# First stage of an RWKV + MoE kernel: whole projections over four PSUM banks instead of halves over two

## The reference

```python
# attention (RWKV time mix)
prev = xn shifted by one step in time
xk, xv, xr, xg = xn + (prev - xn) * tm_k, tm_v, tm_r, tm_g
r = xr @ Wr.T;  k = xk @ Wk.T;  v = xv @ Wv.T;  g = sigmoid(xg @ Wg.T)
wkv = scan over time of exp(k), exp(k) * v with a decay per channel
o = (sigmoid(r) * wkv * g) @ Wo.T, then a layer norm
# ffn: RMS norm to z, a router (softmax, top 4 of 32 experts, at most 256 tokens each),
# the experts' gated MLPs, and a shared gated MLP of width 1408
```

## Time and profile before

| | |
|---|---|
| median of 3 runs | 1800.13 us (1799.75 to 1804.7) |
| the profiled execution | 1803.59 us, its span 1801.8 us |
| busy over the span | PE 94%, DVE (VectorE) 69%, POOL 49%, ACT 37% |
| mean granted clock of TensorE | 0.979 |
| first stage | 0 to about 484 us |
| second and third stage | to about 949 us, and to the end |

### The profile page before, as it was taken

The page is one execution under the profiler, slowest core; times in us unless marked ns, Lnnn a source line. Parts: engine busy times, 40 slices in busy tenths (PEclk is TensorE's granted clock), DMA queues, the critical chain, the costliest instruction groups (busy, mean ns, idle before and its releaser), DMA issues. The chain is left out here.

```text
span 1801.8 us, 26943 instructions
## 1 busy us (share of the span) xinstructions
PE 1687.4 (94%) x8752; PEld 1445.2 (80%) x8752; DVE 1247.5 (69%) x1798; ACT 661.2 (37%) x1083; POOL 874.2 (49%) x727
## 2 busy tenths in 40 slices
PE   4899999999599999999986889999999999999998
PEld 4687887778489999999974778888788888888887
DVE  4888787888255555555545868778686868777776
ACT  3444445444256656656642322112121211212121
POOL 2678777777634444454423524344252524334251
PEclk9999999999889999999998999999999999999999
DMA  6233334333366676676637655455454443343431
GB/s 222 94 137 129 133 140 160 120 117 117 120 249 217 242 249 221 234 251 228 228 110 263 211 203 170 156 187 172 165 165 140 151 147 106 113 163 117 141 107 51
DMA packets 130475, 299.43 MB, mean 166 GB/s; under 512 B 23692, under 2 KB 35212, under 8 KB 129872
## 3 DMA queue, kind: packets, MB, share of 16 engines
q1 hardware_dynamic: 110928, 264.64, 41.5%
q0 software_dynamic: 19456, 33.67, 6.6%
HBM read 233.64 MB, written 81.36 MB: 175 GB/s over the span
## 5 line engine op out<-in xcount | busy, mean ns | idle before, releaser
L738 PE MATMUL pj<-mix,w 128*128 128x512 f32 x1536 | 368.4, 397 | 18.6 <-POOL mix L311 18.4
L738 PEld LDWEIGHTS pj<-mix,w 128*128 128x128 f32 x1536 | 287.6, 190 | 85.2 <-POOL mix L311 14.6
L1616 PE MATMUL s_gp<-s_zT,s_wg 128*128 128x512 f32 x1056 | 263.7, 400 | 37.6 <-DVE s_wg L1524 21.9
L1616 PEld LDWEIGHTS s_gp<-s_zT,s_wg 128*128 128x128 f32 x1056 | 203.9, 194 | 84.4 <-DVE s_wg L1524 24.8
L1630 PE MATMUL s_yp<-s_wd,s_h 128*128 128x512 f32 x1056 | 255.2, 391 | 2.9 <-DVE s_h L1433 2.9
L1616 PE MATMUL s_up<-s_zT,s_wu 128*128 128x512 f32 x1056 | 253.7, 389 | 0.0
L1630 PEld LDWEIGHTS s_yp<-s_wd,s_h 128*128 128x128 f32 x1056 | 199.2, 189 | 44.7 <-issue 3.3
L1616 PEld LDWEIGHTS s_up<-s_zT,s_wu 128*128 128x128 f32 x1056 | 198.2, 188 | 41.4
L876 POOL TENSOR_TENSOR e_wg<-e_g_in,e_wg 128x1408 fp32r<-128x1408 f32 x32 | 103.4, 3233 | 214.6 <-ACT e_wg L896 214.6
L311 POOL TENSOR_TENSOR mix<-mixf,mix 128x512 fp32r<-128x512 f32 x128 | 175.8, 1403 | 61.1 <-ACT mix L385 60.9
L1275 POOL DMA_INDIRECT s_picked<-y_rows,s_slot x128 | 143.4, 1121 | 85.0 <-DVE s_total L1483 47.4
(11 more groups left out here) (148 smaller groups left out, 2377.5 us busy)
## 6 DMA issues: line engine op xcount, KB each, us to landing
s_wu<-wu_split SPq DMA_DIRECT2D x77, 512.0 KB, 3.5
e_g_in<-in_w_gate SPq DMA_DIRECT2D x32, 704.0 KB, 4.5
e_u_in<-in_w_up SPq DMA_DIRECT2D x32, 704.0 KB, 5.9
zT_tiles<-zT SPq DMA_DIRECT2D x32, 512.0 KB, 2.6
e_d_in<-in_w_down SPq DMA_DIRECT2D x32, 512.0 KB, 6.8
y_rows<-e_y SPq DMA_DIRECT2D x32, 512.0 KB, 2.9
s_zT<-zT_tiles SPq DMA_DIRECT2D x32, 512.0 KB, 5.6
x_in<-in_x SPq DMA_DIRECT2D x32, 256.0 KB, 4.1
```

Source lines behind the costliest of these rows:

```text
L738: last = pe.matmul(pj[m][:], w[i][:, w_part, k, m * P:(m + 1) * P], mix[:, i % 2, k, x_part, :], start=(k == 0 and q == 0), stop=(k == KC ...
L1616: last = pe.matmul(bank[:], parts[w_part][:, k, :], zT[:, :, x_part, k, :], start=(q == 0 and k == 0), stop=(q == 2 and k == KC - 1))
```

## The change

On TensorE `project` no longer takes a half. Chunk by chunk it now runs the three matmuls of all four banks, so that each chunk feeds 12 matmuls in a row and the first chunk asks for all four banks. The count, the turns and the scores stand only between projections: the count and the turns of tiles 0 and 1 between V and R; score 0, turns of tile 2, score 1, turns of tile 3 between R and G; scores 2 and 3 between G and K of the next row. Nothing stands between K and V. ACT makes its four `gate_r` in one go, then `keep_turned` 2 and 3, the four `mix_hi` of the next K, and the four `gate_g`. VectorE makes the four mixes of the next K ahead of its four `make_gate`. `gate_g` and `make_gate` of banks 2 and 3 no longer slip into the next round. `exp_k`, `make_xn`, `make_ekv`, `z_lo`, `choose`, `assign` and all of POOL's and SP's order are as they were.

```diff
@@ scalar, one_round
-                if before:
-                    gate_g(b - 1, 2)
-                    gate_g(b - 1, 3)
                 for k in range(KC):
                     mix_hi(b, V_, k)
                 exp_k(b, 0)
...
                 for k in range(KC):
                     mix_hi(b, G_, k)
-                gate_r(b, 0)
-                gate_r(b, 1)
+                for m in range(4):
+                    gate_r(b, m)
                 if more:
                     keep_turned(b + 1, 1 - half, 2)
-                gate_r(b, 2)
-                gate_r(b, 3)
-                if more:
                     keep_turned(b + 1, 1 - half, 3)
-                    mix_hi(b + 1, K_, 0)
-                    mix_hi(b + 1, K_, 1)
-                gate_g(b, 0)
-                gate_g(b, 1)
-                if more:
-                    mix_hi(b + 1, K_, 2)
-                    mix_hi(b + 1, K_, 3)
+                    for k in range(KC):
+                        mix_hi(b + 1, K_, k)
+                for m in range(4):
+                    gate_g(b, m)
@@ vector, one_round
                 if more:
                     norm_stats(b + 1)
-                if before:
-                    make_gate(b - 1, 2)
-                    make_gate(b - 1, 3)
...
                     make_mix(b + 1, 1 - half, K_, 0)
                     make_mix(b + 1, 1 - half, K_, 1)
-                make_gate(b, 0)
-                make_gate(b, 1)
                 if more:
                     make_mix(b + 1, 1 - half, K_, 2)
                     make_mix(b + 1, 1 - half, K_, 3)
+                for m in range(4):
+                    make_gate(b, m)
@@ tensor, project and one_round
-            def project(b, i, pair):
-                if pair == 0 and isinstance(b, int) and b == 0:
+            def project(b, i):
+                if isinstance(b, int) and b == 0:
                     pe.wait_ge(w_lo, i + 1)
                 for k in range(KC):
-                    if pair == 0:
-                        pe.wait_ge(lo_made, b * 16 + i * 4 + k + 1)
-                    for m in (2 * pair, 2 * pair + 1):
+                    pe.wait_ge(lo_made, b * 16 + i * 4 + k + 1)
+                    for m in range(4):
                         if k == 0:
                             taken(b, i, m)
...
-                project(b, K_, 0)
-                project(b, K_, 1)
-                project(b, V_, 0)
+                project(b, K_)
+                project(b, V_)
                 count(b)
                 if more:
                     turn_z(b + 1, 0)
                     turn_xn(b + 1, 0)
-                project(b, V_, 1)
-                if more:
                     turn_z(b + 1, 1)
                     turn_xn(b + 1, 1)
-                project(b, R_, 0)
+                project(b, R_)
                 if more:
                     score(b + 1, 0)
                     turn_z(b + 1, 2)
                     turn_xn(b + 1, 2)
-                project(b, R_, 1)
-                if more:
                     score(b + 1, 1)
                     turn_z(b + 1, 3)
                     turn_xn(b + 1, 3)
-                project(b, G_, 0)
+                project(b, G_)
                 if more:
                     score(b + 1, 2)
                     score(b + 1, 3)
-                project(b, G_, 1)
```

More of the change, by code:

```diff
@@ L455, in one_round @@
                     mix_hi(b, G_, k)
-                gate_r(b, 0)
-                gate_r(b, 1)
+                for m in range(4):
+                    gate_r(b, m)
                 if more:
                     keep_turned(b + 1, 1 - half, 2)
-                gate_r(b, 2)
-                gate_r(b, 3)
-                if more:
                     keep_turned(b + 1, 1 - half, 3)
-                    mix_hi(b + 1, K_, 0)
-                    mix_hi(b + 1, K_, 1)
-                gate_g(b, 0)
-                gate_g(b, 1)
-                if more:
-                    mix_hi(b + 1, K_, 2)
-                    mix_hi(b + 1, K_, 3)
+                    for k in range(KC):
+                        mix_hi(b + 1, K_, k)
+                for m in range(4):
+                    gate_g(b, m)
             rounds(act, one_round)
-            gate_g(B - 1, 2)
-            gate_g(B - 1, 3)
         @block.vector
@@ L676, in one_round @@
                     make_mix(b + 1, 1 - half, K_, 3)
+                for m in range(4):
+                    make_gate(b, m)
             rounds(dve, one_round)
-            make_gate(B - 1, 2)
-            make_gate(B - 1, 3)
         @block.tensor
```

## The result

The changed kernel takes 1832.56 us (median of 4 runs, 1827.01 to 1834.0) beside 1801.03 for the kernel before: 1.0166 times as long, 95% interval 1.014 to 1.0192. The forecast was 1820, slower, in a range of 1808 to 1832: the direction and the main term held, the size was a third too small, and the median lies 0.6 us past the range's end (the ratio, applied to the 1800.13 that the forecast started from, gives 1830). The profiled execution took 1832.38 us, 28.8 more than the profiled one of before.

What follows compares the result with a forecast made beforehand. First stage bound by PE's own work plus 2.8 us a round of POOL waits. Rounds 1 to 6 +11.2, clock +6.5, round 0 +0.5, round 7 +1.8: +20 us, 1820 from 1800.13; range 1808 to 1832.

Steps and rivals of the forecast that it cites:

- What goes: PE's POOL waits ahead of V and within its first half, 2.8 us a round, and three block starts, 0.25.
- R's bank 2: In R's first chunk PE waits for VectorE's ekv 2, behind assign: 3.9 us a round, bounds 3.0 and 5.7.
- The xn copy: Turning xn of tile 1, PE waits for ACT's copy of tile 0 from the one PSUM bank: 0.4 to 0.5 us.
- Table load: ACT's loads ahead of exp and R's sigmoids cost nothing; rival, a drain of some 1380 ns behind the load: 1827, chance 0.02.
- G to K: Between G and the next K, scores of tiles 2 and 3 cover the gates, made within 1.5 us: nothing.
- my rival's mechanism: Slower than forecast: POOL's run holds VectorE in choose, delaying ekv, up to 1.8 us more a round, 1831; chance 0.14.
- just in time: POOL's work for V's first chunk is ready at 44.7, K ends at 44.8: no wait ahead of V.
- two times in three: PE idles of some 3 to 4 us lower its clock, costing 1.6 us each: +6.5 in all, bounds 0 and 10.
- Rounds 0 and 7: Round 0: two idles go, a longer one in R comes, +0.5; round 7: assign begins later after K's start, +1.8.
- The signs: Trace: no POOL wait ahead of V, ekv wait 3.5 to 4.5 us, period 56 to 57.5, first stage 15 to 22 longer.
- faster: Rival: VectorE reaches ekv 2 before PE asks in R, at 3.8; 1788 us, chance 0.05.
- even: Rival: R's wait is 2.4 to 3 us and the clock stays up; 1800 to 1805 us, chance 0.07.

Runs made afterwards that it cites:

- the first ekv fix: The changed kernel with VectorE's four make_ekv together, ahead of zT's low part and assign: 1806.05 us, ratio 1.0023.
- the best kernel of the new form: The changed kernel with four ekv ahead of assign, scatters 12 to 15 behind V's mixes, four exps in one go, VectorE's rounds written out: 1785.45 us, ratio 0.9911.
- V in halves again: The changed kernel with V alone in halves, count and turns of tile 0 between them; K, R and G whole: 1807.5 us, ratio 1.0034.

## Why the prediction was right, and where it was short

- **What goes** held: the 2.3 us ahead of V, and the waits inside it, are gone in four of six rounds (3.4 a round with the block starts, 3.05 forecast).
- **R's bank 2**, the main term, held: 3.9 forecast, 3.70 in the ledger, in all of the steady rounds; the first ekv fix brings 26 us. "Assign beside nothing" was the right thing to look for.
- **The xn copy**: 0.4 to 0.5 forecast, 0.36 measured as a wait, 0.68 with what the turns lose around it. **Exp**: 0.2 forecast, 0.15 to 0.3. **Table load**: ahead of the wait, and 202.96 - 201.66 = 1.30 us from load to sigmoid again; no drain shows, so that rival is out.
- **G to K** was booked at nothing and cost 0.31 a round. The cover I named, the two scores, is there, but VectorE's last mix of K was late: held through POOL's run of three (6.60 us for four mixes where two took 1.40), and ACT's gates queue behind that mix. That is my rival's mechanism, VectorE held by POOL, at another place; where I had put it, in choose, it cost nothing that PE saw. The Trainium skill (SBUF — State Buffer, on the shared port pair) has it that a VectorE operation with two SBUF inputs and a GpSimd one that reads SBUF shut each other out for a whole instruction. These rows agree, and they show more: VectorE got in only when the whole run of three, 3.79 us, was over.
- **POOL, "just in time: 0, bounds 0 and 1 us"** is the first step that failed. In rounds 3 and 5 it was 1.9 to 2.0 us late, with 1.7 for the clock: 7.3 us. The walk took VectorE's norm_stats to begin right behind the gates; at the loop's head it began 2.15 us later. The rows of the kernel before could not warn of that: there norm_stats of round 3 begins at 210.54, as the mixes ahead of it end, and POOL asks for it five us after it is done. What else differs is the order at the loop's end (two mixes of K there, four gates that wait for ACT here); whether that lets the jump come through was not tested.
- **The clock, "two times in three"**, is the second: it fell in six steady rounds of six, 10 us instead of 6.5. A count of three stalls of other lengths and places was too thin for a fraction, and the third, the 3.8 us ahead of K in round 0, was misread (below).
- Gates, turns and exps were 1.3 us a round where 0.7 was booked, 3.6 us in six rounds; R's wait, 0.2 shorter, and what goes, 0.35 more, gave about as much back.
- Rounds 0 and 7, +0.5 and +1.8 forecast, were +1.2 each. In round 0 the two idles did not simply go: PE stood 3.10 us for the xn copy there, and 5.33 for ekv.
- **The signs**: I had called myself wrong "if POOL still holds V". It does in rounds 3 and 5. The periods, 57.8 to 58.0 and 61.5, lie above the 56 to 57.5 named, and the stage grew by 32.3 us, not 15 to 22. That the time still lies at the range's end is in part luck: the untouched stages took 3.5 us less.
- The **faster** and **even** rivals needed R's wait below 3 us; it was 3.7.

The misread stall: windows behind the 3.8 us ahead of K of round 0, first of the kernel before, then of the changed kernel.

```profile
37.50:40.90 3.40, 3.39 (x8) 2.73 (x9) 0.90 (x2) 2.43 (x2) 3.40 (x3) 1.00 0.00 0
37.60:41.00 3.40, 3.38 (x8) 2.73 (x9) 0.90 (x2) 2.43 (x2) 3.40 (x3) 0.50 0.02 5
```

The granted clock reads 1.00 in the first and 0.50 in the second, but both get 8 matmuls through in 3.4 us, where 15 go through at full clock. By its pace, then, the kernel before ran the start of K at the lower level too, and its longest stall is no case of a clock that stayed up. What the column says should be held against the count of matmuls beside it.

## What to carry to other kernels

When a step is made to ask for all of a resource at once instead of half, look at what the other engines do between the first and the second half of the hand-over: an order that was hidden behind the first half becomes a stall without one line of it changed. Then walk the next-late chain too: here three things (ekv, POOL's scatters, a loop's jump) were within 4 us of each other, an edit to one of them alone was worth 26, 0 or 12 us, and two together 46. And try the cheap edit on the chain that ends the wait before reshaping the engine that waits: moving four scatters in the old kernel gave all that the best kernel of the new form gave.

## What the runs showed of the hardware that I had not expected

The length of a stall does not tell by itself whether TensorE's clock falls behind it. It fell after 1.88 us twice (V in halves again), after 1.94, 1.97 and 2.01 us ahead of V, and after 3.4 to 3.6 ahead of bank 2, six times of six; it did not fall after five of 2.3 in the kernel before (two of them in the earlier trace rows). Behind 3.13 us in the kernel with VectorE written out it fell once and stayed up twice. Most falls cost 1.6 to 1.7 us, a few 2.6. What decides was not settled; filling the stall with 2.7 us of spare matmuls kept the clock up in all six steady rounds and paid for itself.

Where a pass of the loop begins, VectorE stood idle for 2.15 and 2.22 us in the changed kernel (4.4 us in its waits), and for 2.2 to 2.8 us in the other kernels of whole projections that keep its loop. It shows in a profile only as "issue" ahead of the first instruction of a pass, and it is gone where the rounds are written out. It does not belong to every loop: in the kernel before, with the same loop, nothing of it shows.
